# A graph attention layer on one core: numerators scaled into the gathered rows, one 260-column product per tile, and the next step's exponentials directly behind the copy of sums

## What is computed

```python
z = (x @ W).reshape(n, HEADS, ODIM)
el = jnp.sum(z * al, axis=-1)
er = jnp.sum(z * ar, axis=-1)
e = jax.nn.leaky_relu(el[src] + er[dst], negative_slope=0.2)
e_max = jax.ops.segment_max(e, dst, num_segments=n)
ex = jnp.exp(e - e_max[dst])
denom = jax.ops.segment_sum(ex, dst, num_segments=n)
alpha = ex / denom[dst]
out = jax.ops.segment_sum(z[src] * alpha[:, :, None], dst, num_segments=n)
out = jax.nn.elu(out + x + b)
```

## Time and profile before

| what | us |
|---|---|
| median of 3 runs (4824.91 to 4829.48) | 4825.26 |
| the profiled execution, first to last instruction | 4824.0 |
| TensorE matmul busy | 3342.4 (69%) |
| TensorE weight loads busy | 2406.6 (50%) |
| VectorE busy | 2350.8 (49%) |
| ScalarE busy | 1279.2 (27%) |
| GpSimd busy | 2537.5 (53%) |

### The profile page before, as it was taken

One profiled execution on the slowest core, in us unless ns is written; L12 is line 12 of the kernel. 1 busy time (PEld: TensorE's weight loads), 2 busy tenths in 40 slices (PEclk: granted clock), 3 DMA queues, 4 the chain that ended last, 5 costly groups with the idle time before them and its releaser, 6 DMA issues. The chain is left out here.

```text
span 4824.0 us, 104766 instructions
## 1 busy us (share of the span) xinstructions
PE 3342.4 (69%) x33932; PEld 2406.6 (50%) x33933; DVE 2350.8 (49%) x7219; ACT 1279.2 (27%) x4694; POOL 2537.5 (53%) x2630
## 2 busy tenths in 40 slices
PE   6567766676667775677777776666576776767676
PEld 4334444444444444455555555555455555555555
DVE  6445444444544444445444444444344554444455
ACT  5112211212212212233333333323222222222232
POOL 6444444444444443555555555553655555555553
PEclk9777777777777777555555555555555555555555
DMA  7222222222222222333333333332333333333332
GB/s 231 78 79 83 78 75 80 80 79 81 81 78 81 77 80 84 88 99 94 94 98 93 98 96 94 96 94 75 96 93 102 94 94 94 97 99 93 94 93 82
DMA packets 241750, 442.92 MB, mean 92 GB/s; under 512 B 83665, under 2 KB 134933, under 8 KB 241567
## 3 DMA queue, kind: packets, MB, share of 16 engines
q0 software_dynamic: 119808, 334.13, 25.4%
q1 hardware_dynamic: 121887, 108.14, 7.3%
HBM read 381.95 MB, written 60.10 MB: 92 GB/s over the span
## 5 line engine op out<-in xcount | busy, mean ns | idle before, releaser
L1655 POOL DMA_INDIRECT nodes<-z_rows,scratch x1664 | 1644.4, 988 | 1272.8 <-issue 415.7
L1101 POOL DMA_INDIRECT scratch<-h_rows,scratch x832 | 818.8, 984 | 941.7 <-DVE nodes L1251 716.0
L1732 PE MATMUL ge_part<-nodes,scratch 128*32 128x64 f32 x13312 | 472.6, 313 | 243.2 <-DVE scratch L1927 133.5
L1624 ACT COPY scratch<-ge_part 128x260 f32<-128x260 f32 x208 | 78.3, 376 | 1851.5 <-remote 1665.8
L1145 PE MATMUL ce_part<-nodes,scratch 128*32 128x128 f32 (+1 forms) x6656 | 456.7, 394 | 126.2 <-issue 113.4
L1732 PEld LDWEIGHTS ge_part<-nodes,scratch 128*32 128x32 f32 x13312 | 359.4, 167 | 296.5 <-issue 153.2
L1145 PEld LDWEIGHTS ce_part<-nodes,scratch 128*32 128x32 f32 x6656 | 256.5, 140 | 331.5 <-issue 279.2
L1279 DVE TENSOR_TENSOR nodes<-nodes,ce_sum 128x512 f32 x105 | 72.3, 689 | 707.6 <-remote 367.0
L1737 PE MATMUL ge_part<-scratch 128*32 128x4 f32 x3328 | 209.9, 200 | 261.5 <-issue 259.3
L1746 PE MATMUL ge_sum<-scratch 128*128 128x128 f32 x832 | 243.6, 445 | 208.4 <-ACT scratch L1624 208.2
L1919 DVE TENSOR_TENSOR scratch<-scratch,ge_runs 128x32 f32<-128x32 f32 x208 | 44.0, 212 | 692.4 <-remote 675.5
(11 more groups left out here) (269 smaller groups left out, 5802.1 us busy)
## 6 DMA issues: line engine op xcount, KB each, us to landing
nodes<-z_rows,scratch POOLq DMA_INDIRECT x1664
nodes<-hT SPq DMA_DIRECT2D x56, 256.0 KB
scratch<-h_rows,scratch POOLq DMA_INDIRECT x832
z_rows<-scratch SPq DMA_DIRECT2D x28, 264.0 KB
z_rows<-nodes SPq DMA_DIRECT2D x28, 264.0 KB
hT<-scratch SPq DMA_DIRECT2D x28, 256.0 KB
hT<-nodes SPq DMA_DIRECT2D x28, 256.0 KB
nodes<-x_rows SPq DMA_DIRECT2D x28, 256.0 KB
```

The costliest lines, as they stand in the source:

```text
L1101: nc.gpsimd.indirect_dma_start(xg[u][:, i * D:(i + 1) * D], None, m.h_rows, bass.IndirectOffsetOnAxis(ap=idx[r][:, k:k + 1], axis=0)).then ...
L1655: nc.gpsimd.indirect_dma_start(zg[r][:, k * ZW:(k + 1) * ZW], None, m.z_rows[layer], bass.IndirectOffsetOnAxis(ap=idx[r][:, k:k + 1], axis ...
L1732: ins = nc.tensor.matmul(ps_part[j * TW:(j + 1) * TW, h * HF:(h + 1) * HF], weighted(k, h), zg[r][:, k * ZW + h * HF:k * ZW + (h + 1) * HF ...
```

## The change

The weights `ex` are no longer multiplied into one-hot matrices. ScalarE writes them into the gathered rows in place of `el` (columns 256 to 259 of each tile), and the 256 features of each row are multiplied in place by their head's weight. One product per tile of the bare one-hot matrix with these 260 columns then gives both sums. `hots` and `ex` go. VectorE scales the four even tiles in one operation (128x4x256) and tile 1 in another (128x256); ScalarE scales tiles 3, 5 and 7 in twelve operations of 64 columns. VectorE and ScalarE no longer wait for `part_summed` of the step before ahead of this. ScalarE takes the exponentials of step v + 1 directly behind the copy of sums of step v.

```diff
+            def exponentials(v, r, u):
+                act.wait_ge(diff_ready, v + 1)
+                nc.scalar.activation(numerators(r), lanes(diff[u]), ACT.Exp).then_inc(ex_ready, 1)
+                nc.scalar.activation(fac[u][:, :], fd[u][:, :], ACT.Exp).then_inc(ex_ready, 1)
+            exponentials(0, 0, 0)
...
-                act.wait_ge(diff_ready, v + 1)
-                nc.scalar.activation(ex[u], diff[u], ACT.Exp).then_inc(ex_ready, 1)
-                nc.scalar.activation(fac[u][:, :], fd[u][:, :], ACT.Exp).then_inc(ex_ready, 1)
...
-                act.wait_ge(part_summed, v + 4)
                 act.wait_ge(ex_ready, v * 2 + 2)
-                for k in range(G // 2 + 1, G, 2):
+                for k in range(3, G, 2):
                     for h in range(HEADS):
-                        ins = nc.scalar.activation(weighted(k, h), one_hot(r, k), ACT.Copy,
-                                                   scale=ex[u][:, h * (G + 1) + k:h * (G + 1) + k + 1])
+                        at = k * ZW + D + h
+                        ins = nc.scalar.activation(head_rows(r, k, h), head_rows(r, k, h), ACT.Copy,
+                                                   scale=zg[r][:, at:at + 1])
...
                 nc.scalar.copy(sums, ps_part[:, 0:D + HEADS]).then_inc(sums_ready, 1)
+                if ahead >= 1:
+                    exponentials(v + 1, (r + 1) % 4, 1 - u)
...
-                for h in range(HEADS):
-                    for j in range(NB):
-                        k = 2 * j + q
-                        ins = nc.tensor.matmul(ps_part[j * TW:(j + 1) * TW, h * HF:(h + 1) * HF], weighted(k, h),
-                                               zg[r][:, k * ZW + h * HF:k * ZW + (h + 1) * HF],
-                                               start=(q == 0 and h == 0), stop=(q == 1), skip_group_check=True)
                 for j in range(NB):
                     k = 2 * j + q
-                    ins = nc.tensor.matmul(ps_part[j * TW:(j + 1) * TW, D:D + HEADS], one_hot(r, k),
-                                           lanes(ex[r % 2])[:, k, :], start=False, stop=(q == 1), skip_group_check=True)
+                    ins = nc.tensor.matmul(ps_part[j * TW:(j + 1) * TW, 0:D + HEADS], one_hot(r, k),
+                                           zg[r][:, k * ZW:k * ZW + D + HEADS], start=(q == 0), stop=(q == 1),
+                                           skip_group_check=True)
...
-            def weighted_one_hots(r, half, q=0):
+            def scale_rows(r, first, last):
+                by_tile = zg[r].rearrange("p (k w) -> p k w", w=ZW)[:, first:last:2]
+                rows = by_tile[:, :, 0:D].rearrange("p k (h f) -> p k h f", h=HEADS)
+                by = by_tile[:, :, D:D + HEADS].rearrange("p k (h o) -> p k h o", o=1)
+                return V.tensor_tensor(rows, rows, by.broadcast_to([P, len(range(first, last, 2)), HEADS, HF]), ALU.mult)
...
                 dve.wait_ge(ex_ready, v * 2 + 1)
-                dve.wait_ge(part_summed, v + 4)
-                weighted_one_hots(r, 0)
-                weighted_one_hots(r, 1).then_inc(hots_ready, 1)
+                scale_rows(r, 0, G).then_inc(rows_scaled, 1)
                 if ahead >= 1:
                     over_tiles(v + 1, 1 - u)
                 scale_first(v - 1, 1 - u, base)
-                weighted_one_hots(r, 0, 1).then_inc(hots_ready, 1)
+                scale_rows(r, 1, 2).then_inc(rows_scaled, 1)
```

More of the change, by code:

```diff
@@ L1405, in gat_stage @@
         hot = [scratch(G * TW) for r in range(4)]
-        hots = scratch(G * HEADS * TW)
         hotT = scratch(2 * P)
@@ L1425, in gat_stage @@
         diff = [scratch(LANES) for u in range(2)]
-        ex = [scratch(LANES) for u in range(2)]
         node = Mem()
@@ L1463, in gat_stage @@
          er_ready, raw_ready, score_ready, eT_ready, ends_ready, lv_ready, state_ready, ini_ready, init_ready, fwd_ready,
-         max_ready, maxT_ready, diff_ready, ex_ready, hots_ready, hots_act_ready, half_summed, part_summed, sums_ready, scaled,
+         max_ready, maxT_ready, diff_ready, ex_ready, rows_scaled, rows_act_ready, half_summed, part_summed, sums_ready, scaled,
          summed, added) = [
@@ L1722, in tile_sums @@
             def tile_sums(v, r, q):
-                pe.wait_ge(hots_ready, v * 2 + (q + 1))
+                pe.wait_ge(rows_scaled, v * 2 + (q + 1))
                 if q == 0:
@@ L1919, in differences @@
                 V.tensor_tensor(lanes(diff[u]), lanes(score[u]), lanes(ps_max), ALU.subtract).then_inc(diff_ready, 1)
-            def weighted_one_hots(r, half, q=0):
-                tiles = slice(half * NB // 2, (half + 1) * NB // 2)
-                out = hots.rearrange("p (a q h n) -> p a q h n", q=2, h=HEADS, n=TW)[:, tiles, q]
-                one = hot[r].rearrange("p (q a o n) -> p a q o n", q=2, o=1, n=TW)[:, tiles, q]
-                by = ex[r % 2].rearrange("p (h e o) -> p e h o", h=HEADS, o=1)[:, q:G:2][:, tiles]
-                return V.tensor_tensor(out, one.broadcast_to([P, NB // 2, HEADS, TW]),
-                                       by.broadcast_to([P, NB // 2, HEADS, TW]), ALU.mult)
+            def scale_rows(r, first, last):
[3 more added lines that the diff above has]
+                return V.tensor_tensor(rows, rows, by.broadcast_to([P, len(range(first, last, 2)), HEADS, HF]), ALU.mult)
             def scale_first(v, u, base):
```

14 lines of the change are left out of this document (8 added, 6 removed).

## The result

The changed kernel takes 4776.99 us (median of 5, 4770.90 to 4798.86) where the kernel before takes 4825.26 in the same set: ratio 0.9897, 95% interval 0.9873 to 0.9922. Measured again in another set of runs, in which the kernel before took 4844.56, it was 0.9938 (0.9919 to 0.9958). The forecast was 4346, range 4125 to 4640. The sign was right; the size was off by a factor of ten: 48 us gained, 479 forecast.

What follows compares the result with a forecast made beforehand. Bound: TensorE instructions that must complete in GpSimd's pauses. A step of 13.63 - 2.46 = 11.17, taken as 11.2 us, saves 2.4 x 199 = 480; 4824.0 - 480 = 4344, plus 1.3 gives 4346 us, range 4125 to 4640.

Steps and rivals of the forecast that it cites:

- The mechanism named: In the edge-group loops, the number of TensorE instructions that must complete in GpSimd's pauses bounds a step, measured 13.6 us.
- the price of an instruction: TensorE in the loops: 128 fewer instructions a step, at 52 per us, save 2.46 us of GpSimd's pauses.
- The rate under the gathers: TensorE completes 5.8 instructions per us while GpSimd gathers, so eight gathers of 10.08 us let 58 through.
- What is late next: GpSimd's pauses after the change: one of 1.88 us shrinks towards 0.30, the other, ahead of q = 0, stays.
- The floor: A loop step without gathers, read from the last eight steps of a layer: 5.6 us each.
- rival 1: GpSimd's gathers become the loops' bound, no pause remains: steps of 10.1 to 10.5 us, 4122 to 4201 us; chance 0.22.
- VectorE's wider operation: Scaling ahead of the q = 0 sums: one operation of 1.22 us against 0.76 for a pair, 0.46 more a step.
- ScalarE's scalings: Twelve operations for eight take 2.7 to 3.4 us a step, 0.9 to 1.6 more; counted as zero.
- The move of the exponentials: ScalarE's exponentials come about 1 us earlier in a step, hiding VectorE's 0.46 us, which uncovered is 92 us.
- Rival 2: Completions in the loops are held up by time, both pauses stay: steps 13.0 to 13.6 us, 4700 to 4824; chance 0.12.
- rival 3: TensorE's wide products do not overlap: a half costs 4.3 us, not 1.1; 4985 us; chance 0.08 with other losses.
- a price of about 60 ns an instruction: Skill's rule for TensorE, given less weight: 98 instructions would take 6.1 us a step and GpSimd would bound.

Runs made afterwards that it cites:

- part 3: Changed kernel with its gathers left out (4055.91 us), replaced by plain transfers (4059.49) or GpSimd zero writes (4077.36), or cut to 66 values a row (4814.69).
- split65: Changed kernel with each 260-column product cut into four of 65 columns, 64 instructions a half in place of 16; ratio 0.9961 to the kernel before.
- narrow: Changed kernel with each product cut to 68 of its 260 columns, same number of instructions; ratio 1.0076 to the kernel before.
- gap: Changed kernel with a 128x256 write of zeros on GpSimd, and a wait for it, behind every gather; ratio 0.9624 to the kernel before.
- gap_split65: Changed kernel with products cut into four of 65 columns and a 128x256 write of zeros behind every gather; ratio 0.9961 to the kernel before.
- part 4: Gathers left out of the kernel before (4022.25 us) and of the changed kernel with the exponentials put back to the head of the step (4046.65 us).
- nogather: Changed kernel with no gathers in the two graph attention loops, GpSimd only raising the semaphores; 4055.91 us.
- part 5: GpSimd writes of zeros behind every gather or every second one, in the changed kernel, edits of it and the kernel before; ratios 0.9515 to 1.0009.

## Why the prediction was wrong

**The mechanism named was there.** "TensorE's completions, not its array, are slow while GpSimd issues gathers" held in every run with gathers and in none without, and part 3 ties it to the indirect gathers. Only "not its array" is half the truth: in the even half of the kernel before TensorE itself stopped beginning instructions. That their number counts, and not their columns, also held: `split65`, `narrow`, and `gap` against `gap_split65`.

**The step that failed is the price of an instruction.** The forecast priced the 128 instructions removed at 52 per us: "At 52 per us that is 2.46 us of GpSimd's pauses". The runs gave 0.25 (part 4). Two readings stood behind it, and both were wrong:

1. *The rate under the gathers was taken as steady*, 5.8 per us, so that "Eight gathers are 10.08 us and let 58 through". Even the earlier trace rows did not have it: eight of its 16 instructions were seen at once, and the other eight took 1.86 us, 4.3 per us. In the timeline of the changed kernel a release 4 us into the gathers is on time, and then 14 instructions need 6.1 us, 2.3 per us; and the next two take another 1.5 us, after the last gather, so that 52 per us is not the rate of every pause either. That the two rates together met the measured step within 0.3 us shows less than it seemed to: the second had been worked out from the same step.

   In the kernel before 80 instructions meet the gathers at once and are late after 2 us. Taken over 1120 us of each trace, from the start of a run of gathers to the first TensorE semaphore over 0.35 us late, the median is 2.0 us and 88 instructions before, 2.7 us and 71 in `split65`, 5.7 us and 45 in the changed kernel (57 of 163, 4 of 126 and 15 of 89 runs of gathers show no late one).

   A hold-up that begins only after a while, and then stops TensorE's own instructions, looks like a room for reports that fills up. But if TensorE's reports alone filled it and it drained meanwhile, more of them would go in the longer it lasts, and there are fewer. So something else fills it too, or it is another thing; no run shows which, nor in what part of the chip. Whether the recording of the profile has a share stays open as well. Every run here is recorded, and under the gathers the record itself has holes: of the 53 updates of L1697's semaphore between 3480 and 4200 us of the kernel before it holds 5, and in `nogather` none is missing.
2. *"What is late next" was answered for GpSimd's pauses only.* I saw that the first pause would close, and booked it as gain. But the gathers then run eight in a row, 9.8 us for 4.7, and the hand-offs behind the sums (the transposes for ScalarE and VectorE, the sums over windows) come to lie in their second half, where reports are late. Before, the transposes had got through in the pause: the two engines waited 0.8 and 6.3 us for them in 20 steps. What is won at the sums is lost again there, in the 7.10 us that GpSimd waits at 4016.57.

**The floor was read in the wrong place.** The forecast took 5.6 us as a step without gathers, from the last steps of a layer. `nogather` shows 9.6, and the earlier trace rows had it: 981 us of matmul busy in 99.1 steps. It did not carry the sum, but it made rival 1 look 4 us better than it was: even with every semaphore on time, the floor is near GpSimd's own.

**The small terms.** VectorE's wider operation (1.21 us, forecast 1.22) and ScalarE's scalings (3.0 us a step, forecast 2.7 to 3.4) had their sizes right, and their cover was nearly there: without gathers the chain grew by 0.12 us a step. The move of the exponentials, booked as a gain of cover, costs 0.5 to 1.1% under gathers.

**The rivals.** Rival 2 (the hold-up goes by time, 4700 to 4824) holds the measured 4777 and its reason was half right: what is lost does not follow from the number removed. But it is not the time either, as part 5 shows. I had given it 0.12, against the earlier trace rows, where small groups are seen at once in the middle of gathers; that row was the start of the rule, not an argument against a hold-up that returns later. Rival 1 and rival 3 did not occur: the eight wide matmuls start within 1.1 us. In this kernel a price of about 60 ns an instruction is not there: 32 matmuls start within 1.08 us, and without gathers 226 instructions a step take no longer than 98. The Trainium skill, "TensorE: Matmul & The Clock Gate" (section "Wait — 56ns, not 53.3ns?"), states its 62 ns for each matmul, with hardware decode off; the prediction charged it to weight loads too. For the matmuls alone I estimate from it 7.0 us a step before and 3.0 after, and the trace does not agree even so, with at most 34 ns for each of those 32.

## What to carry to other kernels

Where an engine's semaphores are late only beside another engine's activity, ask how much of the held-up work must pass in each stretch of it: here taking instructions out of one hand-off moved the wait to the next one, and a pause that broke the stretch was worth more. Here a write of zeros that lasts half a microsecond behind every second gather gained 3.2% on the changed products (0.9515 against 0.9827), over three times what the change did by itself. And a floor is read from a full step with the suspected activity taken out, not from the last steps of a loop.

## What was unexpected

- TensorE's semaphores come 3.4 to 4.9 us behind the modelled end in the rows shown, while GpSimd issues indirect gathers (0.96 us each, every 1.26), and never over 1 us late with plain transfers of 135 GB/s or with GpSimd writing zeros.
- A GpSimd that does more is faster: 128x256 zeros (0.33 us) behind each gather, pause 0.50 for 0.30 us, take 2.8 to 3.2% off the kernel with 98 TensorE instructions a step and nothing off the one with 226. A write of 128x8 (0.125 us) leaves the pause at 0.30 and gains nothing (0.9924 against 0.9827 without it, 1% slower, which stays unexplained).
- Less work can be slower: products of 68 columns for 260 gave 1.0076 against 0.990 to 0.994.
